# Graph layers with 36 buffers for fetched rows and gathered tiles in fewer batches

## The chip, the cores and the metric

One core of one Trainium2 chip runs the whole kernel. The metric is the time of one execution on the device in microseconds, median of three runs: 1799.24 (1791.07 to 1801.76).

## The reference

The graph has 3125 nodes with 256 features and 50,000 edges, sorted by destination. With `norm[e] = dis[src] * dis[dst]` (from the degrees), three layers follow:

```python
def tagconv(x, src, dst, norm, W, b):
    out = x @ W[0]
    h = x
    for k in range(1, 4):
        h = segment_sum(norm[:, None] * h[src], dst, N)
        out = out + h @ W[k]
    return out + b
h = relu(tagconv(x, ..., W1, b1)); h = relu(tagconv(h, ..., W2, b2))
return layernorm(x + tagconv(h, ..., W3, b3))
```

## The kernel before, in words

**The form of the work.** The adjacency commutes with the weights, so a layer is evaluated as a nested sum: V3 = g W3, then three hops, V(k) = g W(k) + A V(k+1) for k = 2, 1, 0. Each value is held as a pair of float16 halves, high and low, so a row of V has 512 columns. There are 25 tiles of 128 nodes (the last has 53 rows). A hop is called (L, k), with layer L = 0, 1, 2; k = 3 is the first projection of a layer. The nine hops follow one another, since each needs all of the V before it.

**Dense and gathered tiles.** In a hop, 19 tiles (`DENSE`, indices 0 to 18) are dense: four projection matmuls (L1266, L1268) and then 25 matmuls of the adjacency in fp8 against V in SBUF (L1405, and L1410 for the last block). Tile 24, which has few rows, is dense too, with its own operand AT (L1383 to L1387), except in the three hops of `LONG`, (0,2), (0,0) and (1,0), where it is gathered. Tiles 19 to 23 are always gathered. Their edges are taken in steps: five steps a tile (`GV`), four windows of 128 edges a step, each window serving 32 destination rows. A window needs 128 rows of V: an indirect DMA on GpSimd's queue (L942) fetches them from the copy of V in HBM (`vh`) into a slot of the buffer GB. TensorE multiplies them by a one-hot selection SG (L1319; L1316 for tile 24), four matmuls of 32 columns side by side, one for each window. The fifth step of a tile needs only two fetches, since two windows share one, so a tile is 18 fetches; tile 24 is 9. A hop has 90 fetches, a long one 99.

**The order.** `schedule()` writes out one list for all engines. In it the gathered steps stand in batches behind dense tiles: the tables `FIRST` (hop (0,2)), `LONGER` (the other long hops), `LAST` (hop (2,0)) and `STEPS` (the rest) say behind which dense index how many steps of `sequence` are done. In hop (0,2) the order of steps is tiles 19, 20, 24, 21 to 23; in the other long hops tile 24 comes first. Behind each dense tile of a hop with k = 0 the list also has the transposition ("T") and the first projection ("P", L+1, 3) of tiles that are finished, for the next layer.

**Fetches.** GpSimd's loop issues the fetches in the order of the steps. It starts a hop once the 25 tiles of V of the hop before are stored by SyncE (`keep`, L700; semaphores `s_vd`). `ring()` deals out the slots of GB in turn; a fetch waits until the step that used its slot before is done on TensorE. There are 24 slots, of which 16 are in use in hop (0,2), as the other 8 hold comparison patterns until then. On TensorE each gather matmul waits for the semaphore of its slot.

**PSUM.** Bank 7 takes each gathered tile (its projection, then its steps). Dense tiles rotate over banks 0, 1, 2, 5, 6 (in (0,2) over 0, 1, 2). Before a bank is used again `emptied()` waits for VectorE. In layer 0 the projection of a tile ("S", `started`, L1285, L1291) is done inside the dense tile before, and ScalarE scales it in place (L977); `gather` waits for that. In layers 1 and 2 `gather` projects a tile itself, at its first step.

**Behind a tile** ScalarE scales the low half (L1120), VectorE adds (L1789), ScalarE writes the high half of V (L1090) and VectorE the low half (L1761), and VectorE takes maxima for a later check of ranges (L1632). In the last hop (2,0) VectorE forms the output (L1837, L1839; L1831, L1833 for the last tile) and the layer normalisation, with a chain of small operations from L1843 to L1859 and two steps on ScalarE (L1135, L1031). The 23rd and 24th tile in the order share one such chain (`members`). ScalarE takes up the next tile after it has scaled the output of the one before.

## Time and profile before

| | us |
|---|---|
| median of three runs | 1799.24 |
| lowest, highest | 1791.07, 1801.76 |
| span of the profiled execution | 1250.4 |
| TensorE busy | 1224.4 (98%) |
| GpSimd busy | 850.6 (68%) |
| VectorE busy | 629.7 (50%) |
| ScalarE busy | 397.2 (32%) |
| granted TensorE clock, mean | 0.993 |

The profile page gives one execution from its first to its last instruction, the span. The time of a run is longer than that; the page does not give the whole time of the execution that it profiles, so its span stands beside the median of the runs, 548.8 us above it. Engines are named PE (TensorE, with PEld for its weight loads), DVE (VectorE), ACT (ScalarE), POOL (GpSimd) and SP (SyncE). L1319 is line 1319 of the kernel before. Times in rows are microseconds from the span's start, unless a column says ns.

### The profile page before, as it was taken

What the parts mean: (1) busy time and instruction counts of PE and PEld (TensorE: products, weight loads), DVE (VectorE), ACT (ScalarE), POOL (GpSimd) and SP (SyncE); (2) the same over time, 40 slices, a digit from 0 to 9 for tenths busy, and PEclk for the clock granted to TensorE, in tenths of its full rate; (3) what the DMA queues carried; (4) which work ended last, traced back from release to release, by engine and by line L of the source; (5) the groups of instructions that cost most, each with busy time, mean ns of one, the idle gap of its engine ahead of it and who ended that gap; (6) DMA issues with size and microseconds to landing.
All of it is one profiled execution on the core that took longest, in us unless ns stands there. A gap on an engine that the chain in (4) does not pass through costs nothing.

```text
span 1250.4 us, 19518 instructions
## 1 busy us (share of the span) xinstructions
PE 1224.4 (98%) x7413; PEld 610.2 (49%) x7413; DVE 629.7 (50%) x1552; ACT 397.2 (32%) x916; POOL 850.6 (68%) x937
## 2 busy tenths in 40 slices
PE   5999999999999999999999999999999999999997
PEld 4655554444444444444444454444444544454444
DVE  7876664444455555433443345555433433345655
ACT  6676774422233331111221122222111111112222
POOL 8677775777477755776577657773777477747773
PEclk8999999999999999999999999999999999999999
DMA  5343443544255553444354435553444344435553
GB/s 182 111 124 107 115 124 101 156 135 135 79 142 157 146 126 104 131 130 125 108 156 132 122 97 150 149 149 94 131 130 128 102 129 130 131 92 151 153 162 93
DMA packets 110070, 160.05 MB, mean 128 GB/s; under 512 B 43719, under 2 KB 82225, under 8 KB 109970
## 3 DMA queue, kind: packets, MB, share of 16 engines
q0 software_dynamic: 40480, 110.54, 31.6%
q1 hardware_dynamic: 69416, 48.13, 12.8%
q8 instruction: 61, 1.00, 0.3%
q14 instruction: 39, 0.32, 0.1%
q10 hardware_dynamic: 74, 0.05, 0.0%
HBM read 120.51 MB, written 32.10 MB: 122 GB/s over the span
## 4 chain that ended last, share of the span: by engine, by line
PE 88%; POOL 5%; DVE 3%; issue 2%; ACT 1%; DMA 1%; POOLq 0%; DVEq 0%; ACTq 0%
PE pb L1405 65%; PE pb L1266 6%; POOL GB L942 4%; PE pb L1319 4%; PE pb L1268 3%; PE pb L1285 3%; PE pb L1161 2%; PE pb L1410 1%; PE pb L1291 1%; PE pb L1383 1%; PE pb L1194 0%; DVE V L1744 0%; POOL gT L825 0%; DMA GB<-vh,KS 0%; DVE gT L1503 0%
## 5 line engine op out<-in xcount | busy, mean ns | idle before, releaser
L942 POOL DMA_INDIRECT GB<-vh,KS x837 | 807.9, 965 | 371.2 <-issue 246.2
L1405 PE MATMUL pb<-V,A 128*128 128x512 f16 x4104 | 944.8, 379 | 0.0
L1405 PEld LDWEIGHTS pb<-V,A 128*128 128x128 fp8e4 x4104 | 395.3, 98 | 429.5 <-issue 5.2
L1789 DVE SCALAR_TENSOR_TENSOR pb<-pb,cst,t 128x256 f32<-128x256 f32 (+1 forms) x200 | 97.7, 488 | 357.8 <-ACT t L1120 357.8
L1120 ACT ACTIVATE t<-pb,cst 128x256 f32<-128x256 f32 (+1 forms) x224 | 105.2, 469 | 441.8 <-PE pb L1410 398.0
L1266 PE MATMUL pb<-Whl,gT 128*128 128x512 f16 x384 | 134.2, 380 | 1.2 <-DVE gT L1730 1.2
L1761 DVE SCALAR_TENSOR_TENSOR V<-V,pb 128x256 f16<-128x256 f16 (+1 forms) x200 | 83.8, 421 | 82.1 <-ACT V L1090 81.5
L1090 ACT ACTIVATE V<-pb 128x256 f16<-128x256 f32 (+1 forms) x200 | 75.9, 383 | 127.3 <-DVE pb L1789 127.2
L1268 PE MATMUL pb<-Whl,gT 128*128 128x256 f16 x384 | 104.7, 273 | 0.0
L1632 DVE TENSOR_REDUCE stat<-V 128x1 f32<-128x256 f16 x225 | 91.3, 412 | 0.2
L1780 DVE TENSOR_REDUCE ast<-A 128x1 f32<-128x610 uint8 x100 | 77.8, 778 | 0.0
L1010 ACT ACTIVATE A<-pb 128x500 fp8e4<-128x500 f32 x122 | 71.1, 585 | 18.2 <-PE pb L1161 17.4
L1794 DVE SCALAR_TENSOR_TENSOR w<-bb,cst,t 128x256 f32<-128x256 f32 (+1 forms) x50 | 24.2, 485 | 80.4 <-ACT t L1120 80.4
L1266 PEld LDWEIGHTS pb<-Whl,gT 128*128 128x128 f16 x384 | 37.5, 98 | 55.0 <-issue 10.3
L1319 PE MATMUL pb<-GB,SG 128*32 128x512 f16 x900 | 58.8, 381 | 0.3 <-DMA GB<-vh,KS 0.3
L977 ACT ACTIVATE pb<-pb,cst 128x512 f32<-128x512 f32 (+1 forms) x75 | 48.5, 650 | 28.3 <-PE pb L1291 28.1
L1161 PE MATMUL pb<-GB,Whl 128*128 128x125 f16 x499 | 50.8, 225 | 2.1 <-DVE GB L1613 1.8
L1161 PEld LDWEIGHTS pb<-GB,Whl 128*128 128x128 f16 x499 | 38.6, 100 | 29.1 <-issue 5.0
L1410 PE MATMUL pb<-V,A 128*128 128x256 f16 x171 | 46.6, 273 | 0.0
L1611 DVE TENSOR_TENSOR Whl<-Whl,GB 128x1024 f16<-128x1024 f16 x63 | 43.4, 688 | 4.4 <-PE pb L1161 3.8
L1285 PE MATMUL pb<-Whl,gT 128*128 128x512 f16 (+1 forms) x150 | 44.5, 379 | 0.3 <-ACT AT L1010 0.3
L1120 ACT ACTIVATE t<-pb 128x256 f32<-128x256 f32 (+1 forms) x50 | 19.1, 382 | 80.3 <-PE pb L1410 73.5
(227 smaller groups left out, 687.8 us busy)
## 6 DMA issues: line engine op xcount, KB each, us to landing
vh<-V SPq DMA_DIRECT2D x216, 128.0 KB
GB<-vh,KS POOLq DMA_INDIRECT x837, 2.8
xr<-in_x SPq DMA_DIRECT2D x24, 128.0 KB, 3.0
out<-g SPq DMA_DIRECT2D x24, 128.0 KB, 1.9
xr<-in_W SPq DMA_DIRECT2D x22, 128.0 KB, 2.4
V<-in_xt SPq DMA_DIRECT2D x5, 512.0 KB, 6.1
gT<-w SPq DMA_TRANSPOSE x46
V<-in_xt SPq DMA_DIRECT2D x1, 640.0 KB, 3.8
```

The costliest lines, as they stand in the source:

```text
L942: pool.indirect_dma_start(GB[:, slot, :], None, vh[vbuf[(L, k + 1)]][:, :], bass.IndirectOffsetOnAxis(ap=KS[:, p:p + 1], axis=0))\
L1120: act.activation(t1[0:r, e % RB, :], lo, ACT.Copy, scale=sc).then_inc(S["s_a1"], 1)
L1161: mm = pe.matmul(BB[gi % 2][:, k * KEYS:(k + 1) * KEYS], OB[:, b % NO, vis % BV // VL, :, vis % VL], OK[:, b % NO, vis % BV // VL, :, vis ...
L1266: pe.matmul(acc[:, :], gT[:, t, c, 0, :], Whl[:, L % 2, c, k, :], start=(c == 0), stop=False, skip_group_check=True)
L1268: mm = pe.matmul(acc[:, F:512], gT[:, t, c, 1, :], Whl[:, L % 2, c, k, 0:F], start=False, stop=(k == 3 and c == 1), skip_group_check=True)
L1285: pe.matmul(high, gT[:, t, c, 0, 0:r], Whl[:, 0, c, k, low], start=(c == 0), stop=False, skip_group_check=True)
L1319: mm = pe.matmul(acc[GH * j:GH * j + GH, :], SG[:, p, :], GB[:, slot, :], start=False, stop=last_step(st), skip_group_check=True)
L1405: mm = pe.matmul(acc[:, :], A8[:, a, t * P:(t + 1) * P], src[:, a, :], start=False, stop=(n == NT - 1), skip_group_check=True)
L1632: dve.tensor_reduce(stat[:, col:col + 1], ap, axis, ALU.max, apply_absolute_value=True).then_inc(S["s_st"], 1)
L1761: dve.scalar_tensor_tensor(lo, vb[0:r, t, 0:F], -SC, hi, ALU.mult, ALU.add).then_inc(S["s_v"], 1)
L1780: dve.tensor_reduce(ast[:, nam:nam + 1], A8[:, a_, NC // 4 * i_:NC // 4 * (i_ + 1)].bitcast(U8), AX.X, ALU.max).then_inc(S["s_st"], 1)
L1789: dve.scalar_tensor_tensor(hi, hi, cst[0:r, 1, t:t + 1], lt, ALU.mult, ALU.add).then_inc(S["s_d1"], 1)
```

## The change

GB gets 36 slots in place of 24, 28 of them in use in hop (0,2) and the 8 lent ones from hop (0,1) on. The room comes from the space for descriptors of dynamic DMAs, which is set to 4096 bytes a partition. The semaphores of six earlier loads serve a second time for slots 30 to 35. The four tables are written anew: hop (0,2) has 6 batches in place of 11, hops (0,0) and (1,0) 4 in place of 6, the other six hops 3 in place of 5. A batch can now hold the steps of two or three tiles; `openers()` lists the tiles that open in a batch, and `gather` projects (or, in layer 0, waits for) all of them at the batch's first step. Gathered tiles alternate between banks 6 and 7 (7 alone in hop (0,2)), and dense tiles rotate over 0, 1, 2, 5. At most two first projections of the next layer stand behind a dense tile; more are left for the next one.

```diff
@@ -45,10 +45,11 @@
 LONG = ((0, 2), (0, 0), (1, 0))
 WG = WIN // GRAN
 FULL = (GV - 1) * WG
-NSLOT, NFIRST = 24, 16
+NSLOT, NFIRST, NLENT = 36, 16, 8
+SCRATCH = 4096
 SGW = 18
-FIRST = {3: 2, 5: 5, 6: 7, 8: 10, 9: 15, 11: 17, 12: 20, 14: 22, 15: 25, 16: 27, 18: 30}
-STEPS = {4: 5, 8: 10, 11: 15, 15: 20, 19: 25}
+FIRST = {4: 5, 7: 10, 8: 15, 11: 20, 14: 25, 18: 30}
+STEPS = {7: 8, 12: 15, 19: 25}
 JZ = 1536
 HP = 125
 HN = N // HP
@@ -65,8 +66,8 @@
 SPREAD = 17
 RULED = 24
 OUTSIDE = 4096.0
-LONGER = {2: 5, 5: 10, 8: 15, 12: 20, 15: 25, 18: 30}
-LAST = {4: 5, 8: 10, 11: 15, 15: 20, 18: 25}
+LONGER = {5: 10, 10: 18, 15: 25, 18: 30}
+LAST = {7: 8, 12: 15, 18: 25}
 LAG = 3
 LATER = (0, 2, 5, 9, 10, 15)
 AHEAD = 9
@@ -138,9 +139,9 @@
                     out += [("S", 0, k, tile_of(st)) for st in sequence(L, k)[at:steps.get(i, at)] if st % GV == 0]
                 out.append(("P", L, k, t))
                 if k == 0 and L < 2:
-                    out += [("P", L + 1, 3, c) for c in fresh]
-                    fresh = done[turned:]
-                    out += [("T", L + 1, c) for c in fresh]
+                    out += [("P", L + 1, 3, c) for c in fresh[:2]]
+                    fresh = fresh[2:] + done[turned:]
+                    out += [("T", L + 1, c) for c in done[turned:]]
                     turned = len(done)
                 done.append(t)
                 for s in sequence(L, k)[at:steps.get(i, at)]:
@@ -203,17 +204,30 @@
 
 def ring(sched):
 
-    slots, use, before = list(range(NFIRST)), {}, {}
+    slots, use, before = [*range(NFIRST), *range(NFIRST + NLENT, NSLOT)], {}, {}
     out = {}
     for L, k, s in (it[1:] for it in sched if it[0] == "G"):
-        if (L, k) == (0, 1) and len(slots) == NFIRST:
-            slots = list(range(NFIRST, NSLOT)) + slots
+        if (L, k) == (0, 1) and len(slots) < NSLOT:
+            slots = list(range(NFIRST, NFIRST + NLENT)) + slots
         for d, _ in fetches(s):
             b = slots.pop(0)
             slots.append(b)
             use[b] = use.get(b, 0) + 1
             out[fetched(L, k) + d] = (b, use[b], before.get(b))
             before[b] = (L, k, s)
+    return out
+
+
+def openers(sched):
+
+    out, run = {}, None
+    for it in sched:
+        if it[0] == "G":
+            run = run or it[1:]
+            if it[3] % GV == 0:
+                out.setdefault(run, []).append(tile_of(it[3]))
+        elif not (it[0] == "P" and it[2] < 3 and it[3] not in dense(*it[1:3])):
+            run = None
     return out
 
 
@@ -576,7 +590,7 @@
         xT = v1.bitcast(F32)
         W3 = g[:, 0:2, :]
         w1 = Whl[:, 1, :, :, :].rearrange("p c k n -> p (c k n)")
-        g2 = GB[:, NFIRST:NSLOT, :].rearrange("p a b -> p (a b)")
+        g2 = GB[:, NFIRST:NFIRST + NLENT, :].rearrange("p a b -> p (a b)")
         OB = w1[:, 0:NO * P * BV].rearrange("p (r u j v) -> p r u j v", r=NO, u=BV // VL, v=VL)
         iotaB = w1[:, 3072:3072 + P * VL].rearrange("p (j v) -> p j v", v=VL)
         KKb = w1[:, 3328:3328 + QK * P]
@@ -611,10 +625,12 @@
             few = (L, k) == (0, 2) or (L, k) == (0, 3) and not 10 <= t < 17
             if (L, k) == (0, 3) and t < len(PAIRED):
                 b = PAIRED[t]
-            elif (L, k, t) == (0, 2, 0) or k < 3 and t not in dense(L, k):
+            elif k < 3 and t not in dense(L, k):
+                b = 6 if (L, k) != (0, 2) and t < NT - 1 and (t - TD) % 2 == 0 else 7
+            elif (L, k, t) == (0, 2, 0):
                 b = 7
             else:
-                b = next(i for i in free if not few or i < 5)
+                b = next(i for i in free if (not few or i < 5) and (i < 6 or (L, k) == (0, 3)))
                 free.remove(b)
                 free.append(b)
             bank_of[e] = b
@@ -649,9 +665,10 @@
         s_x = [sem(f"s_x{i}") for i in range(len(XC) - 1)]
         s_ol = [sem(f"s_ol{i}") for i in range(RB)]
         s_msg = [sem(f"s_msg{i}") for i in range(9 * NQ)]
-        s_gl = [sem(f"s_gl{i}") for i in range(QW + 1)]
+        s_landed = [sem(f"s_landed{i}") for i in range(QW + 1)]
+        s_gl = s_landed
         s_vd = [sem(f"s_vd{i}") for i in range(2)]
-        s_gb = [sem(f"s_gb{i}") for i in range(NSLOT)]
+        s_gb = [sem(f"s_gb{i}") for i in range(NSLOT - len(s_landed))] + s_landed
         split = [w[:, i, :].bitcast(F16).rearrange("p (c h m) -> p c h m", c=2, h=2) for i in range(2)]
 
         def landings(L, t):
@@ -1292,24 +1309,31 @@
                                    skip_group_check=True)
                 mm.then_inc(S["s_pj"], 1)
 
+            OPENED = openers(SCHED)
+
+            def opened(L, k, t):
+
+                e = pe_no[(L, k, t)]
+                if L == 0:
+                    pe.wait_ge(S["s_pm"], s_no[(L, k, t)] + 1)
+                    return
+                emptied(p_of[user[e]])
+                if t == NT - 1:
+                    tail(L, k, PB[e])
+                else:
+                    project(L, k, t, PB[e])
+
             def gather(L, k, st):
 
                 t = tile_of(st)
-                e = pe_no[(L, k, t)]
-                acc = bank[7]
-                if st % GV == 0 and L == 0:
-                    pe.wait_ge(S["s_pm"], s_no[(L, k, t)] + 1)
-                elif st % GV == 0:
-                    emptied(p_of[user[e]])
-                    if t == NT - 1:
-                        tail(L, k, acc)
-                    else:
-                        project(L, k, t, acc)
+                acc = PB[pe_no[(L, k, t)]]
+                for other in OPENED.get((L, k, st), ()):
+                    opened(L, k, other)
                 for j, (d, p) in enumerate(multiplied(st)):
                     if (L, k) == (0, 2):
                         pe.wait_ge(S["s_s5"], 3 + p // SGW)
                     slot, use, _ = RING[fetched(L, k) + d]
-                    pe.wait_ge(s_gb[slot], 16 * use)
+                    pe.wait_ge(s_gb[slot], 16 * (use + (slot >= NSLOT - len(s_landed))))
                     if t == NT - 1:
                         for m in range(2):
                             at = HALF * m + GH * j
@@ -1867,7 +1891,7 @@
     from concourse import mybir as _mybir
     from concourse.bass_utils import run_bass_kernel_spmd as _run
 
-    nc = _bacc.Bacc("TRN2", target_bir_lowering=False, num_devices=1)
+    nc = _bacc.Bacc("TRN2", target_bir_lowering=False, num_devices=1, dynamic_dma_scratch_size=SCRATCH)
     src = _np.asarray(inputs["src"])
     dst = _np.asarray(inputs["dst"])
     pad = _np.full(WIN, -1, _np.int32)
```

## Rows read from the trace of the kernel before

**Rows 1.** Part 1 of the page: busy us (share of the span) and instructions.

```profile
PE 1224.4 (98%) x7413; PEld 610.2 (49%) x7413; DVE 629.7 (50%) x1552; ACT 397.2 (32%) x916; POOL 850.6 (68%) x937
```

**Rows 2.** Stretches: length, then busy us of PE, PEld, DVE, ACT, POOL; clock, DMA.

```profile
60.00:1238.00 1178.00, 1176.12 (x6982) 575.26 (x6981) 574.69 (x1406) 352.61 (x805) 806.89 (x836) 1.00 0.45 128
1238.00:1250.40 12.40, 4.95 (x79) 3.60 (x77) 6.86 (x24) 3.01 (x7) 0.00 (x0) 0.80 0.10 31
```

**Rows 3.** Waits of TensorE for fetched rows: us in total, times, longest us.

```profile
PEld pb L1319 <- DMA GB<-vh,KS: 1.8, 4, 0.8
...
PE pb L1319 <- DMA GB<-vh,KS: 0.3, 1, 0.3
```

**Rows 4.** The fetch line: ns min/median/max of an issue, and us to landing.

```profile
L942 POOL DMA_INDIRECT GB<-vh,KS x837: 940/946/3077, 58.8 to 1233.1; - x168
...
DMA to landing us min/median/max: 2.6/2.8/4.6
```

**Rows 5.** Timeline of PE around a batch in hop (1,2): start us, us, line.

```profile
573.27 0.27 PE L1268 MATMUL pb<-Whl,gT 128*128 128x256 f16 x1
573.47 1.26 PE L1319 MATMUL pb<-GB,SG 128*32 128x512 f16 x20
574.66 0.39 PE L1266 MATMUL pb<-Whl,gT 128*128 128x512 f16 x1
```

**Rows 6.** Timeline of PE: L1405 of two dense tiles in succession.

```profile
575.33 5.34 PE L1405 MATMUL pb<-V,A 128*128 128x512 f16 x24
...
581.26 5.34 PE L1405 MATMUL pb<-V,A 128*128 128x512 f16 x24
```

**Rows 7.** Timeline of PE in (0,2): end of dense tile 8; tile 24's gather.

```profile
119.91 0.27 PE L1410 MATMUL pb<-V,A 128*128 128x256 f16 x1
...
129.23 0.73 PE L1316 MATMUL pb<-GB,SG 128*32 128x256 f16 x20
```

**Rows 8.** Timeline of POOL in hop (0,2): fetches 25, 36 and 45.

```profile
96.34 0.95 POOL L942 DMA_INDIRECT GB<-vh,KS  x1 [3.25 <-PE pb L1319]
...
111.51 0.95 POOL L942 DMA_INDIRECT GB<-vh,KS  x1 [0.30 <-issue]
...
124.30 0.97 POOL L942 DMA_INDIRECT GB<-vh,KS  x1 [0.30 <-issue]
```

**Rows 9.** Timeline of PE: last batch of (0,1), and index 5's of (0,0).

```profile
328.24 1.26 PE L1319 MATMUL pb<-GB,SG 128*32 128x512 f16 x20
...
370.51 1.26 PE L1319 MATMUL pb<-GB,SG 128*32 128x512 f16 x20
```

**Rows 10.** Costliest groups, VectorE's maxima: busy us, mean ns, idle us before.

```profile
L1632 DVE TENSOR_REDUCE stat<-V 128x1 f32<-128x256 f16 x225 | 91.3, 412 | 0.2
```

**Rows 11.** Timeline: first fetches of (0,0) and (1,2), last of (1,2), last batch.

```profile
334.88 0.94 POOL L942 DMA_INDIRECT GB<-vh,KS  x1 [14.98 <-DMA vh<-V]
...
478.23 0.94 POOL L942 DMA_INDIRECT GB<-vh,KS  x1 [18.28 <-DMA vh<-V]
...
589.47 0.95 POOL L942 DMA_INDIRECT GB<-vh,KS  x1 [0.30 <-issue]
...
596.52 1.26 PE L1319 MATMUL pb<-GB,SG 128*32 128x512 f16 x20
```

**Rows 12.** Timelines of DVE and PE at the end, in order of time.

```profile
1225.53 0.16 DVE L1859 SCALAR_TENSOR_TENSOR lnb<-lnb 128x1 f32<-128x1 f32 x1
...
1226.79 0.48 DVE L1837 SCALAR_TENSOR_TENSOR g<-pb,cst,t 128x256 f32<-128x256 f32 x1 [0.73 <-ACT t L1120]
...
1229.65 0.16 DVE L1859 SCALAR_TENSOR_TENSOR lnb<-lnb 128x1 f32<-128x1 f32 x1
...
1237.65 0.27 PE L1410 MATMUL pb<-V,A 128*128 128x256 f16 x1
...
1238.55 0.49 DVE L1837 SCALAR_TENSOR_TENSOR g<-pb,cst,t 128x256 f32<-128x256 f32 x1 [2.58 <-ACT t L1120]
...
1243.75 0.49 DVE L1831 SCALAR_TENSOR_TENSOR t<-pb,cst,w 64x256 f32<-64x256 f32 x1
```


## The prediction

> **What bounds the kernel now.** I read the busy time of each engine first: TensorE is busy for 98% of the span, GpSimd for 68% [rows 1]. An average can hide a stage with another limit, so the second view cuts the span into start, middle and end: between 60 and 1238 us TensorE is busy for 1176.1 of 1178 us, at full clock, and at the end it stops at about 1243 while VectorE works on [rows 2]. The reader is to see that no wait in the middle is worth more than 1.9 us together: time there can be gained only by giving TensorE less to do. The third view is the waits: TensorE has waited for fetched rows for 0.3 us, and its weight loads for 1.8 us, in five places [rows 3]. The fourth is the fetch line on GpSimd: 837 fetches of 0.946 us, one every 1.25 us with the issue gap, each landing 2.8 us (at most 4.6) after its issue [rows 4]. So a hop of 90 fetches takes GpSimd 112 us out of the hop's 126 (19 tiles by 5.94, five gathered ones by 1.94 with projection and change of form, some 3 for tile 24), and it can start only when the hop before is stored. GpSimd is off the path, but by little, and that is where the change can lose what it gains.
>
> The page gives the span of the profiled execution, 1250.4 us, and not its whole time. The median of the three runs is 548.8 us longer. I carry that part unchanged: my sum is a difference of spans, laid on the median of 1799.2.
>
> **Fewer batches.** Before, the gathered steps stand in 53 batches: 11 in hop (0,2), 6 each in (0,0) and (1,0), 5 in each of the other six. After there are 32: 6, 4, 4 and 18. No matmul is added or removed. What goes is the change of TensorE between its 128-column and 32-column forms. In hop (1,2) a batch of 20 gather matmuls starts 0.20 us after a matmul whose own pace is 0.107, and the next projection starts 1.19 us later, while five rounds of four parallel matmuls at 0.213 are 1.07 [rows 5]. So one batch costs 0.10 + 0.12 = 0.22 us beside its work, and 21 batches fewer give **-4.6 us**, all of it on the path, since TensorE is never idle there. [...] The bounds of this term are near: 0.20 to 0.25.
>
> **Waits for rows that go.** In the hops with five batches the first one came after 5 dense tiles and needed 18 fetches; now it comes after 8 and needs 30. A dense tile is 5.94 us [rows 6], so the engine comes 17.8 us later and the fetches 15 us later: 2.8 us of slack more, and likewise for the old third batch. I take **-1.0 us** for this, between the 0.3 and 2.1 of [rows 3]. Later on the slack stays: 54 fetches are now wanted after 13 tiles and not after 12.
>
> **The ring of buffers.** With 36 slots fetch n waits for the use of fetch n-36. In a hop with batches of 30, 24 and 36 fetches the 37th is issued about 5 + 45 = 50 us into the hop, and the first batch runs from 48.8 us on (8 tiles and two projections). The waits are met, or nearly; the last batch needs 36 rows, exactly the ring. I cost this at nothing. Its cover is GpSimd's lead: if it goes, each us of delay comes out in the last batch of the hop.
>
> **Hop (0,2).** Here the lead is short. Tile 24's steps move from dense index 9 to index 8, and they need fetch 45. Before, TensorE did them at 129.2 us and ended index 8 at 120.0 [rows 7]. Now it ends index 8 at about 120.4 (three more gathered steps before it, one batch fewer). Fetch 45 was issued at 124.30, in a stream that had lost 3.25 us to a wait for a slot [rows 8]. With 28 slots in place of 16 that wait goes, so it is issued at 121.05 and lands at 123.9, wanted at 121.0: a stall of 2.8 us, and 0.3 more at index 11, where fetch 63 is wanted. I take **+3.1 us**. Bounds: 0.5 (GpSimd's slower rows, of which this hop has most, fall elsewhere: the issue takes 0.940 at best and 3.077 at worst [rows 4]) to 5 (a landing of 4.6).
>
> **Hops (0,0) and (1,0).** The first batch, at index 5, is now the double one: tiles 24 and 19 on 27 fetches. Hop (0,0) starts at 329.4, where the gather that began at 328.24 ends, and its index-5 batch began at 370.51 [rows 9]. One batch (0.73), one projection of the next layer (0.65) and a 0.1 fall out before it, so it begins at 369.0 and wants its last row at 370.4. GpSimd started at 334.88 [rows 11]. It will start 0.9 us later: three tiles now end almost together before the hop (24, 22, 23) and VectorE needs about 2.6 us for each, six operations of 0.41 to 0.49 like those of [rows 10]. Fetch 27 then lands at 335.8 + 32.8 + 2.8 = 371.4: a stall of 1.0, and 0.2 at index 10. In (1,0) fewer of those operations stand before the start, GpSimd begins about 1 us nearer to it, and I find no stall. **+1.2 us**, bounds 0 and 5 (both hops, landings of 4.6 at each of two batches).
>
> Hop (1,2) has the longest wait for the stores of V, 18.3 us before its first fetch [rows 11]. The 30 fetches of its first batch are issued by 514.5 and landed by 517.3. The hop began near 471.5 (its last gather ends at 597.7, 126 later), so the batch comes at 519: safe by 2 us.
>
> **Two banks, one bank fewer for dense tiles.** Dense tiles rotate through four banks, not five. A bank is drained some 3 us after its tile and asked for again after four tiles, 24 us: nothing. Three ACT scalings instead of two behind tile 24 in layer 0 could hold TensorE 0.2 us once: nothing. At most two projections of the next layer now stand between dense tiles, so they spread and do not grow.
>
> **The end.** VectorE is the path from 1238 on. Tile 18 ends on TensorE at 1237.92; VectorE takes it up at 1238.55 and, tile 23 between, tile 24 at 1243.75 [rows 12]. The pair that shares one normalisation chain is the 23rd and 24th in order: before tiles 18 and 23, after it 22 and 23. Tile 18 then has a chain of its own. Such a lone tile holds up the next one for 4.1 us: 3.02 from 1226.79 to the end of 1229.65's row, and 1.10 from a chain's last row (ends 1225.69) through ScalarE's two steps to the next start at 1226.79 [rows 12]. So after tile 18's end the last tile is taken up at 0.63 + 4.12 + 5.20 = 9.9 us in place of 5.8 (5.20 is the pair, 1238.55 to 1243.75): 4.1 later. Against this, tile 18 itself ends 1.7 us earlier, as tile 22's projection (0.65, 574.66 to 575.33 in [rows 5, 6]) and gather (1.07) move behind it. **+2.4 us**; bounds 0 and 4.
>
> **Sum:** -4.6 - 1.0 + 3.1 + 1.2 + 2.4 = +1.1 us, so 1800.3. [...]
>
> **Rivals.**
> (a) *The whole gain arrives.* No new stall, and the end is hidden: 1799.2 - 5.6 = 1793.6. For it: TensorE is nearly never idle, and my stalls come from margins of 1 us. Against: fetch 45 would have to land 2.8 us sooner, and the end is a plain chain of rows.
> (b) *The fetches fall behind more.* Landings near 4.6 at every double batch and later hop starts carried on: some 1.8 us at each of 5 tight batches beyond my sum, so 1800.3 + 9 = 1809. For it: stores of V move in the same stretches. Against: the median landing is 2.8.
> [...]
> (d) *The change does not do what it says in time*: the 548.8 us outside the span move with the different layout, to either side. Nothing in the profile speaks for it; at 2%, 1763 or 1835.
>
> **How the numbers follow.** My forecast 0.55, (a) 0.24, (b) 0.11, (c) 0.06, (d) 0.04. Adding the bounds gives -6.2 to +9.1, or 1793 to 1808. The three runs lie 8 below and 3 above their median, and a new median can do so too; with (a) and (b) the range is 1788 to 1812. (c) and (d) are left out. One per cent, 18 us, is about what a measurement of this kernel tells from no change. No case but (d) gives faster by 1%: 0.03 with an allowance; (c), half of (d) and the tail of (b) give slower 0.08; within 0.89.
>
> **What would show it.** Right: batches of about 1.7, 1.5 and 2.3 us in the ordinary hops and TensorE's L1319 rows in 32 places; a wait of TensorE for fetched rows near 121 us; the last tile's L1831 about 10 us after tile 18's last matmul, not 6. [...] A median beyond 1812 or under 1788 would break the sum.

## The result, and the profile after

The changed kernel takes 2049.09 us (median of 6 runs, 2044.95 to 2059.12) against 1794.99 us for the kernel before beside it (1791.07 to 1801.76): ratio 1.141, interval 1.1375 to 1.1438. It is 14% slower, where 1800.3 in 1788 to 1812 was forecast.

The profiled execution of it took 2044.95 us for a span of 2043.2. So 1.75 us lie outside the span, and the picture is another than that of [rows 1]: the page's busy row, the granted clock in 40 slices, the engines' share of the chain that ended last, the three groups that matter, and the longest waits of GpSimd (us in total, times, longest).

```profile
PE 1403.7 (69%) x7413; PEld 633.1 (31%) x7413; DVE 628.6 (31%) x1552; ACT 398.6 (20%) x916; POOL 842.9 (41%) x937
...
PEclk8787896887877797877797777869678967896788
...
PE 58%; issue 21%; another core or an unknown queue 13%; DVE 4%; ACT 3%; POOL 1%; DMA 0%; ACTq 0%; POOLq 0%; DVEq 0%
...
L1429 PE MATMUL pb<-V,A 128*128 128x512 f16 x4104 | 1093.2, 408 | 402.1 <-issue 302.9
L959 POOL DMA_INDIRECT GB<-vh,KS x837 | 799.8, 956 | 1142.4 <-PE pb L1343 548.3
L1429 PEld LDWEIGHTS pb<-V,A 128*128 128x128 fp8e4 x4104 | 410.5, 102 | 965.9 <-issue 503.1
```

```profile
POOL GB L959 <- PE pb L1343: 548.3, 20, 42.7
PEld pb L1429 <- issue: 503.1, 535, 3.4
...
POOL GB L959 <- DMA vh<-V: 300.4, 9, 44.8
```

TensorE is busy for 69%, not 98%, and the idle time before the dense matmuls (L1405 before, L1429 now) is put down to "issue": the engine waited for nothing that the profile shows. GpSimd's fetches are as cheap as in [rows 4] (0.956 us); it waits for TensorE's gather (L1343), 20 times.

The timeline shows what happens. TensorE in hop (1,2): start us, us, line, and idle time before.

```profile
906.51 0.27 PE L1285 MATMUL pb<-Whl,gT 128*128 128x256 f16 x1
906.72 1.69 PE L1343 MATMUL pb<-GB,SG 128*32 128x512 f16 x28
908.34 0.39 PE L1283 MATMUL pb<-Whl,gT 128*128 128x512 f16 x1
...
914.94 5.34 PE L1429 MATMUL pb<-V,A 128*128 128x512 f16 x24
...
920.88 0.38 PE L1429 MATMUL pb<-V,A 128*128 128x512 f16 x1
923.35 0.38 PE L1429 MATMUL pb<-V,A 128*128 128x512 f16 x1 [2.09 <-issue]
924.78 0.58 PE L1429 MATMUL pb<-V,A 128*128 128x512 f16 x1 [1.05 <-issue]
...
937.42 0.59 PE L1429 MATMUL pb<-V,A 128*128 128x512 f16 x1 [2.23 <-issue]
938.82 0.58 PE L1429 MATMUL pb<-V,A 128*128 128x512 f16 x1 [0.82 <-issue]
940.22 5.29 PE L1429 MATMUL pb<-V,A 128*128 128x512 f16 x13 [0.81 <-issue]
```

GpSimd at the same time: the first and the last of 24 fetches that it issues 1.25 us apart.

```profile
907.64 0.95 POOL L959 DMA_INDIRECT GB<-vh,KS  x1 [20.97 <-PE pb L1343]
...
936.46 0.94 POOL L959 DMA_INDIRECT GB<-vh,KS  x1 [0.30 <-issue]
```

And the two stretches of that run, cut where TensorE changes pace (length, busy us of PE, PEld, DVE, ACT, POOL; clock, DMA share, GB/s):

```profile
907.64:921.26 13.62, 13.62 (x79) 6.21 (x71) 5.34 (x12) 1.92 (x5) 10.44 (x11) 1.00 0.42 125
921.26:940.20 18.94, 5.64 (x10) 1.14 (x11) 1.71 (x4) 0.38 (x1) 12.32 (x13) 0.57 0.36 104
```

For 13.6 us from the first fetch TensorE runs at full pace. Then its matmuls start 1.4 to 2.8 us apart, in steps of 0.70 us; with the weight load between, that is at best an instruction in 0.70 us. It stays so until the last fetch has landed (936.46 issued, full pace from 940.22), and in 18.9 us it does ten matmuls. The granted clock is 0.57 in that stretch and 0.50 from 924 to 938 us, where TensorE is busy for 4.7 of 14 us. I call it a *slow stretch*, and fetches issued without a pause a *run*. The trace after has 33 runs, of 36, 30 and 24 fetches in an ordinary hop, and nearly every one has its slow stretch.

### The profile page after: what moved, and what is told of

The parts are those of the page before. It is cut to its first block, busy times and chain, and to the rows that moved or that the text cites. A ratio compares the mean times of both kernels' runs of the same rounds, so it can differ in the third digit from the quotient of the medians.

```text
span 2043.2 us, 19514 instructions
## 1 busy us (share of the span) xinstructions
PE 1403.7 (69%) x7413; PEld 633.1 (31%) x7413; DVE 628.6 (31%) x1552; ACT 398.6 (20%) x916; POOL 842.9 (41%) x937
## 3 DMA queue, kind: packets, MB, share of 16 engines
q0 software_dynamic: 40480, 110.54, 19.0%
## 4 chain that ended last, share of the span: by engine, by line
PE 58%; issue 21%; another core or an unknown queue 13%; DVE 4%; ACT 3%; POOL 1%; DMA 0%; ACTq 0%; POOLq 0%; DVEq 0%
PE pb L1429 44%; PE pb L1283 4%; PE pb L1285 2%; PE pb L1343 2%; PE pb L1302 1%; PE pb L1178 1%; PE pb L1434 1%; PE pb L1308 1%; PE pb L1407 1%; ACT t L1137 1%; ACT A L1027 1%; DVE pb L1813 1%; DVE stat L1656 0%; ACT V L1107 0%
## 5 line engine op out<-in xcount | busy, mean ns | idle before, releaser
L1429 PE MATMUL pb<-V,A 128*128 128x512 f16 x4104 | 1093.2, 408 | 402.1 <-issue 302.9
L959 POOL DMA_INDIRECT GB<-vh,KS x837 | 799.8, 956 | 1142.4 <-PE pb L1343 548.3
L1429 PEld LDWEIGHTS pb<-V,A 128*128 128x128 fp8e4 x4104 | 410.5, 102 | 965.9 <-issue 503.1
L1283 PE MATMUL pb<-Whl,gT 128*128 128x512 f16 x384 | 141.0, 396 | 42.1 <-issue 36.8
L1285 PE MATMUL pb<-Whl,gT 128*128 128x256 f16 x384 | 108.4, 282 | 35.8 <-issue 35.5
L1302 PE MATMUL pb<-Whl,gT 128*128 128x512 f16 (+1 forms) x150 | 48.6, 408 | 55.3 <-DVE V L1785 34.9
L1343 PE MATMUL pb<-GB,SG 128*32 128x512 f16 x900 | 54.3, 380 | 0.0
```

What stands on the lines that cost most here:

```text
L959: pool.indirect_dma_start(GB[:, slot, :], None, vh[vbuf[(L, k + 1)]][:, :], bass.IndirectOffsetOnAxis(ap=KS[:, p:p + 1], axis=0))\
L1283: pe.matmul(acc[:, :], gT[:, t, c, 0, :], Whl[:, L % 2, c, k, :], start=(c == 0), stop=False, skip_group_check=True)
L1285: mm = pe.matmul(acc[:, F:512], gT[:, t, c, 1, :], Whl[:, L % 2, c, k, 0:F], start=False, stop=(k == 3 and c == 1), skip_group_check=True)
L1343: mm = pe.matmul(acc[GH * j:GH * j + GH, :], SG[:, p, :], GB[:, slot, :], start=False, stop=last_step(st), skip_group_check=True)
L1429: mm = pe.matmul(acc[:, :], A8[:, a, t * P:(t + 1) * P], src[:, a, :], start=False, stop=(n == NT - 1), skip_group_check=True)
```

## The experiments

Theory A: a run of GpSimd's fetches leaves TensorE about 14 us at full pace and slows it from there until the run has landed. The execution profiled of the kernel before had no slow stretch although its fetches ran for 112 us without a pause; its ordinary executions would have them, and the 548.8 us are inside their span.

**The kernel before, once more.**

> The kernel before, unchanged, for a profile of an ordinary execution: the profiled one had a span of 1250.4 us, the timed ones took 1795. Theory A (crawl): once GpSimd has issued fetches without a pause for some 14 us, TensorE gets its instructions only every 0.7 us until the last of them has landed; the lost time goes by the length and number of these runs of fetches. It then expects a span near 1793, a mean clock near 0.85, about 46 stretches of slow TensorE in 46 runs of fetches, each beginning 13 to 15 us after a run begins, and each run ending in a wait of GpSimd for a slot. Theory B (descriptor space): the kernel before has no such stretches; a span near 1250 beside a run time of 1795 would then mean that 545 us lie outside the span.

1797.05 us, span 1795.3. Its busy row and clock; then one run of 18 fetches from 896.23, cut as above.

```profile
PE 1404.6 (78%) x7413; PEld 637.4 (36%) x7413; DVE 629.6 (35%) x1552; ACT 398.3 (22%) x916; POOL 845.6 (47%) x937
...
PEclk8998998888797898889888988889887988897879
```

```profile
896.23:910.90 14.67, 14.53 (x79) 6.55 (x71) 6.51 (x14) 3.95 (x11) 11.32 (x12) 1.00 0.51 147
910.90:921.00 10.10, 3.93 (x10) 0.73 (x9) 0.00 (x0) 0.00 (x0) 5.95 (x7) 0.74 0.34 100
```

The same picture. The ordinary execution of before has 54 runs (24, 18, 18, 18, 12 in a hop; 46 in all were expected). The trace that the prediction read was not one of them.

**The descriptor space alone**, in the kernel before:

```diff
+nc = _bacc.Bacc("TRN2", ..., dynamic_dma_scratch_size=4096)
```

> The kernel before with the descriptor space of dynamic DMAs set to 4096 bytes, and nothing else: 24 buffers, old batches. Theory A: no change, 1795 within 1%. Theory B: the smaller space is what costs, so about 2049, and at least a third of the 254 us.

1789.83 us, ratio 0.9965 (0.9946 to 0.9983). The smaller space costs nothing, and GpSimd's 784 gaps before a fetch that the profile puts down to "issue" are 0.3 us at most: rival (c), by which the smaller space holds GpSimd up, falls.

**The buffers without the tables**: the changed kernel with `FIRST`, `STEPS`, `LONGER` and `LAST` of before.

> The changed kernel with the four tables of batches of the kernel before: 36 buffers, 4 KB, two banks, 53 batches. Theory A: with 36 buffers the first run of a hop grows from 24 to 36 fetches and the number of runs in a hop falls from 5 to 4, in nine hops; each pause saved costs about 12 us (254 us for 21 batches), so about 1900. Theory T (the tables alone, with the long batches and their double projections): 1795. Theory B: 2049.

1883.12 us, ratio 1.0485 (1.045 to 1.052). With 36 slots the first run of a hop is 36 long and swallows the second: 36, 18, 18, 18, some 44 runs. So about a third of the loss comes with the buffers (this kernel also keeps the change of banks and the limit of two first projections behind a dense tile, which no run takes alone), two thirds with the tables, which make it 33 runs.

**Runs cut to 9**, in the kernel before:

```diff
                             .then_inc(s_gb[slot], 16)
+                        run += 1
+                        if run % DRAIN == 0:
+                            pool.wait_ge(s_gb[slot], 16 * use)
```

> The kernel before, and GpSimd waits after every ninth fetch of a hop until that fetch has landed, before it issues the next. Theory A: runs of 9 fetches last 11 us and end before the slow stretch would begin; a pause of 3 us may be long enough to renew the start. Then a hop is bound by GpSimd, 10 times (11.3 + 2.8) = 141 us and its start, nine hops about 1330 and 65 before them: about 1400. If a pause of 3 us is too short: 1795 or somewhat more. Theory B and any theory in which fetches are only late: GpSimd loses 25 us in each hop, so slower than 1795, near 1850.

1489.35 us, ratio 0.8296 (0.8273 to 0.8319), with one added wait on GpSimd, though not the 1400 us that were reckoned: from one hop to the next it takes 144 to 184 us. Its busy row; GpSimd around a pause; the run of nine between two pauses:

```profile
PE 1315.2 (89%) x7413; PEld 620.4 (42%) x7413; DVE 630.9 (43%) x1552; ACT 396.8 (27%) x916; POOL 850.6 (58%) x937
```

```profile
738.20 0.95 POOL L943 DMA_INDIRECT GB<-vh,KS  x1 [0.30 <-issue]
741.23 0.95 POOL L943 DMA_INDIRECT GB<-vh,KS  x1 [2.09 <-issue]
```

```profile
728.20:741.20 13.00, 12.98 (x76) 6.06 (x78) 4.73 (x10) 2.72 (x8) 8.51 (x9) 1.00 0.47 132
```

A pause of 3.0 us from issue to issue, and TensorE keeps its pace. Same matmuls, same fetches: what cost the time was the unbroken run.

**The changed kernel with the same wait.**

> The changed kernel whole (36 buffers, 4 KB, longer batches, two banks), and in it GpSimd waits for the landing of every 9th fetch of a hop before it issues the next, as in the kernel before with that wait, which took 1489.35 us. Theory A (what the change costs is only that GpSimd's unbroken runs of fetches get longer, and TensorE issues an instruction in some 0.7 us from about 14 us into a run until it has landed): with all runs cut to 9 fetches the two kernels come out nearly alike, 1465 to 1515 us, the difference being the small terms of my sum (+1.1 us, between -7 and +10). Rival R (the longer batches themselves hold TensorE up, since buffers come free later and its first matmul waits longer): the changed kernel stays over 5% behind, 1570 us or more.

1486.69 us, ratio 0.8245 (0.8206 to 0.8284): level with the kernel before under the same wait, whose interval it overlaps. Rival R falls here: with runs of the same length the 14% are gone.

**Every 6th and every 3rd**, in the kernel before (`DRAIN = 6`, `DRAIN = 3`).

> The kernel before, with GpSimd waiting for the landing of every 6th fetch in place of every 9th (1489.35 us). Theory A: the short slow stretches that were left with 9 (some 110 us of idle TensorE in them) mostly go, since a run of 6 lasts about 6.3 us and is landed at 9; each pause costs GpSimd some 1.8 us, 15 of them in a hop in place of 10, 9 us a hop on an engine that has slack in most hops. 1400 to 1480 us. Rival Q (it is not how long a run lasts, the waits helped only because they moved the fetches to another place against the batches): no clear gain on 9, 1480 to 1560 us.

1459.35 us, ratio 0.8122 (0.8091 to 0.8152), in the range. Before the dense matmuls no idle time is put down to "issue" any more (208.0 us in the ordinary execution of before, 48.6 with every 9th). What TensorE waits for now is rows: 88.1 us in 94 waits.

> The kernel before, with GpSimd waiting for the landing of every 3rd fetch. Theory A: no slow stretch is left (a run of 3 is landed 5 us after its first issue), but GpSimd now needs 3.8 us x 30 = 114 us and 30 pauses of 1.8 us = 54 us in a long hop, 168 us against the 147 us that a hop takes with every 9th, so GpSimd is the bound: 1500 to 1620 us with the mean granted clock of TensorE no lower than with 9 (0.95). Rival Q: slow stretches go on, the clock stays below 0.95.

1710.52 us, ratio 0.9513 (0.948 to 0.9546): above the range, and the clock was 0.881, not 0.95. Now TensorE waits for rows far more than the 2.1 us of [rows 3]. The gather matmuls, and GpSimd's fetches:

```profile
L943 POOL DMA_INDIRECT GB<-vh,KS x837 | 805.7, 963 | 835.0 <-DMA GB<-vh,KS 577.4
...
L1323 PE MATMUL pb<-GB,SG 128*32 128x512 f16 x900 | 167.0, 438 | 265.6 <-DMA GB<-vh,KS 264.5
```

GpSimd is the bound: from the first to the last fetch of an ordinary hop it takes 162 to 167 us, as reckoned (168). What I left out are the 8 us until the next hop can start (16 behind (0,0) and (1,0)) and the 20 to 30 more that hops (0,2), (0,0) and (1,0) take. The clock fell where TensorE waits for rows: 0.74 from 720 to 740 us, with 8.7 us of such waits, and 1.00 from 740 to 760, where it is always busy. Before TensorE's dense matmuls the profile has no idle time from "issue", so there are no slow stretches.

**A wait two behind**: after each issue GpSimd waits for the landing of the fetch two before it.

```diff
+                        sent.append((slot, use))
+                        if len(sent) > 2:
+                            pool.wait_ge(s_gb[sent[-3][0]], 16 * sent[-3][1])
```

> The kernel before, and from the third fetch of a hop on GpSimd waits, after each issue, for the landing of the fetch issued two before it. At most three are ever under way, but the queue never runs empty as long as a run lasts (a landing comes about 2.8 us after its issue, and issues are 1.25 us apart). Theory A1 (what counts is that the queue runs empty now and then): slow stretches as before, 1750 to 1850 us. Theory A2 (what counts is a backlog of fetches that builds up in a run until it holds up TensorE's instructions): no backlog can build up, the slow stretches go, and the time comes to 1400 to 1520 us.

1749.52 us, ratio 0.9728 (0.9696 to 0.9759). The added wait hardly ever holds GpSimd up (the profile puts 8.4 us in 11 waits down to landings): in a run it goes on issuing 1.25 us apart, so each fetch has landed by the time that it is asked for. The slow stretches stay, and no backlog of fetches is behind them (A2 falls). Why this kernel is 2.7% faster is not shown.

**What starts a slow stretch.** Two kernels leave work out, a third issues the dense columns in twice as many instructions:

```diff
 # every second gather matmul left out, the last step excepted
+                    if j % 2 == 0 and not last_step(st):
+                        continue
 # 64 rows a fetch from a slot's second use on
+                        rows = P if use == 1 else P // 2
+ pool.indirect_dma_start(GB[0:rows, slot, :], ..., ap=KS[0:rows, p:p + 1])
 # each dense matmul as two of 256 columns
+                            for m in range(2):
+                                mm = pe.matmul(acc[:, F * m:F * (m + 1)], ..., src[:, a, F * m:F * (m + 1)], ...)
```

> The kernel before, and in a gathered tile's steps but the last TensorE leaves out every second matmul (12 of 20 in a tile are left, so its output is not the reference's). Fetches, waits and batches are as before. Asked is what starts a slow stretch. Theory T (the time or the number of fetches since a run of GpSimd began): slow stretches start 13 to 15 us and some 11 fetches into a run, as before, though fewer of TensorE's instructions lie between. Theory I (the number of TensorE's instructions since then, 120 to 150 in the runs before, as if a store of fetched instructions were used up that isn't filled again while fetches go on): they start later by about the share left out, at 18 us or more, and the short runs of 12 and 18 show none.

1742.28 us (one run; before beside it 1757.44). It could not tell: so few of the instructions of a run are gather matmuls that the slow stretch came after as many as before, at 16.4 us. That short runs would show none was a miss.

> The kernel before, and a fetch into a buffer that has been used before brings 64 rows in place of 128 (rows 64 to 127 of the buffer keep what they held, so the output is not the reference's). Half the descriptors and half the bytes a fetch; GpSimd's time for one should fall from 0.95 us. Theory D (the descriptors or bytes queued are what starts and feeds a slow stretch): a slow stretch starts only after some 22 fetches of a run, so that runs of 12 and 18 show none, and within one TensorE's instructions come faster than one in 0.7 us; total well below 1700 us. Theory T (time since the run began): starts at 13 to 15 us whatever the fetch brings. Theory N (the number of instructions on GpSimd's queue): starts after 11 fetches, earlier in time.

1821.1 us (one run; before beside it 1757.44). Half the rows and half the bytes a fetch (57.26 MB on the fetches' queue in place of 110.54) gain nothing, and the slow stretch starts as early as before: D falls.

> The kernel before, with each dense 128x512 matmul (4104) issued as two of 256 columns, each with its weight load: the same columns multiplied in twice as many of TensorE's instructions, GpSimd's fetches as before. Theory T (the time since a run of GpSimd's fetches began, 13 to 15 us): slow stretches start where they did, 13 to 15 us in. In them an instruction still takes some 0.7 us, so the stretches, whose end GpSimd sets, get half as many columns done. Total 1800 to 1950 us. Theory I (the number of TensorE's instructions since the run began: it was 110 to 177 in every slow stretch of the runs so far, at 0.1 us each mostly, and where TensorE waited between, 25 or 30 us passed before it was reached): slow stretches start when some 140 of the doubled instructions are through, 7 to 9 us and 6 to 8 fetches into a run, the runs of 12 are slow too, and each of some 50 runs costs 6 us more on top: 2050 to 2400 us.

2044.77 us (one run; before beside it 1761.44), 5 us under the range of theory I. One run of each, up to the slow stretch and into it, in this order:

```profile
914.50:930.90 16.40, 16.16 (x81) 7.31 (x77) 5.23 (x11) 1.90 (x5) 12.45 (x14) 1.00 0.42 120
930.90:939.50 8.60, 2.67 (x7) 0.81 (x8) 0.00 (x0) 0.00 (x0) 4.52 (x5) 0.69 0.32 91
```

```profile
949.67:963.50 13.83, 13.83 (x77) 6.37 (x69) 5.23 (x11) 1.90 (x5) 10.47 (x12) 1.00 0.29 81
963.50:975.00 11.50, 3.72 (x8) 0.80 (x8) 0.00 (x0) 0.00 (x0) 5.71 (x7) 0.70 0.15 41
```

```profile
1494.34:1502.20 7.86, 7.86 (x74) 6.06 (x66) 3.29 (x7) 1.05 (x3) 6.03 (x7) 1.00 0.42 119
1502.20:1519.00 16.80, 6.26 (x24) 2.09 (x23) 0.49 (x1) 0.74 (x2) 11.02 (x12) 0.59 0.36 101
```

The last pair decides. With twice as many instructions the stretch starts at 7.9 us and 7 fetches, not at 14.7 and 12, but after about as many of TensorE's instructions: 74 + 66 = 140 against 79 + 71 = 150. Theory I holds, T falls, and so does N, a count of fetches. The median over the runs from hop (1,2) on, instructions counted by their starts, says much the same (where exactly a slow stretch starts can be read within 1 us): 14.6 us and 140 instructions before, 13.6 and 143 after, 16.2 and 153 with gather matmuls left out, 13.9 and 134 with half rows, 7.9 and 128 split. The small differences fit a store that in a run goes down by one for each instruction and is made up by one in 0.70 us, the pace of the slow stretch. From the rows: 150 - 14.67/0.70 = 129 for the kernel before, 140 - 7.86/0.70 = 129 for the split one, 131 for the changed kernel, 126 for half rows, 135 for the kernel with matmuls left out. That is a model that fits five kernels, not a thing seen.

**A shorter pause**: the wait after every 9th fetch is for the 8th.

> The kernel before, and after every 9th fetch of a hop GpSimd waits for the landing of the 8th, not of the 9th: a pause of some 1.9 us from issue to issue in place of 3, and the 9th fetch is still under way when the wait ends, so the queue is hardly ever empty. If only an empty queue lets TensorE's instructions be fetched again (A1): as without a wait, 1730 to 1820 us. If a pause of GpSimd itself is enough (A3): as with the full wait or better, 1440 to 1520 us.

1637.46 us, ratio 0.931 (0.9238 to 0.9381; before beside it 1761.44), between both theories. The pause is 1.70 us from issue to issue (731.82 to 733.52). It is neither that only an empty queue helps nor that any pause will do; in the model, a shorter pause makes up part of the store.

**The changed kernel with every 6th.**

> The changed kernel, with GpSimd waiting for the landing of every 6th fetch. With every 9th the changed kernel (1486.69 us) and the one before (1489.35 us) came out alike; with every 6th the one before took 1459.35 us. Theory A, by which the change costs nothing but longer runs: alike again, 1445 to 1475 us. If 36 buffers let GpSimd get ahead where it is what is waited for (it is 34% of the chain of waits there): 1435 to 1455 us. Rival R (the longer batches cost by themselves where GpSimd is close to being the bound): over 1475 us.

1492.16 us, ratio 0.8465 (0.8406 to 0.8525; before beside it 1761.44). The kernel before had 1459.35 with this wait, ratio 0.8122, with 1798.26 beside it. So by times the changed kernel is 2% slower and by ratios 4%, and the time lies in rival R's range. TensorE waits 113.2 us for rows, 25 more than the kernel before with this wait, and in hop (0,0) another 10.3 us, in five waits, for VectorE to empty a bank. The starts of the hops (first fetch, us from one hop to the next) show where:

```
                       (0,2) (0,1) (0,0) (1,2) (1,1) (1,0) (2,2) (2,1)
before, every 9th      184.2 155.7 172.2 143.8 145.7 171.1 144.7 147.3
changed, every 9th     196.1 147.2 194.7 141.6 143.4 180.9 140.4 143.1
before, every 6th      169.2 148.6 171.2 145.1 147.3 170.1 145.7 145.5
changed, every 6th     175.8 149.5 174.9 150.6 153.9 174.8 149.1 148.5
```

By these rows long hops seem to like the old tables and short runs, ordinary hops the new tables and runs of 9. The next kernel puts that to the test.

**Each hop its better form**: the changed kernel with the old `FIRST` and `LONGER`, and waits by hop.

```diff
+DRAIN = {(0, 2): 6, (0, 0): 6, (1, 0): 6}
+                        if run % DRAIN.get((L, k), 9) == 0:
```

> The changed kernel with a wait for every 9th fetch in the six ordinary hops and for every 6th in (0,2), (0,0) and (1,0), and with the batch tables FIRST and LONGER of before for these three. From the hops' starts in the traces: with the changed tables and every 9th the ordinary hops take 140.4 to 143.4 us (143.8 to 147.3 with the tables of before, 148.5 to 153.9 with every 6th), while the three long ones are shortest with the old tables and every 6th (169.2, 171.2, 170.1 against 196.1, 194.7, 180.9). Added up, 58 + 169 + 147 + 171 + 142 + 143 + 170 + 140 + 143 + about 150 for the last hop and the end = 1433. If the parts add (theory A: a hop's time is that of its own runs and batches): 1415 to 1450 us. If hops are not independent (how many of TensorE's instructions are left over from the hop before decides): 1460 us or more.

1447.15 us, ratio 0.8064 (0.8036 to 0.8092), in the range, but the parts did not add as I had it. From one hop's first fetch to the next the ordinary hops take 139.3 to 145.7 us, as reckoned. The long ones take 176.0, 176.0 and 175.7, not 169, 171 and 170, and the changed kernel with the new tables and every 6th had 175.8, 174.9 and 174.8. So the tables are not what makes the long hops longer. What is left is the rest of the change, the slots, the banks and the limit on first projections, and no run separates these. One place shows in the trace, again in hop (0,0), where L1306 is the projection that the kernel before has in L1285 (us in total, times, longest):

```profile
PE pb L1306 <- DVE V L1789: 10.2, 5, 2.7
```

The kernel beats the one before by 19%. It had the lowest time, but its interval touches that of the kernel before with every 6th (0.8091 to 0.8152), which needs only the added wait. Its busy row:

```profile
PE 1297.4 (90%) x7413; PEld 624.3 (43%) x7413; DVE 632.6 (44%) x1552; ACT 397.3 (27%) x916; POOL 849.7 (59%) x937
```

## Why the prediction was wrong

**The step that failed** is the one ahead of the sum: "I carry that part unchanged". It took the 548.8 us between span and median for something outside the work, and the profiled execution for a picture of the rest. The runs show that an ordinary execution of before spans 1795.3 us, 1.75 below its own time, 545 us more than the trace that I read: TensorE is idle for 365 us more of them and busy for 180 more, at a lower clock, with slow stretches in most of its runs. Rival (d) named the gap and gave it 0.04, because nothing in the profile spoke for a move. But a span 30% short of the runs was itself the sign: the trace could not show where a third of the time went, and a range of 1788 to 1812 had no ground.

**"I cost this at nothing. Its cover is GpSimd's lead"** The ring is where the loss enters. Fetching goes on for 837 x 1.25 = 1046 us however it is cut, and each run gives TensorE only its first 14 us. Longer batches and 36 slots give fewer, longer runs: 54, 44, 33. One hop, (1,1), before and after, has the same busy time of TensorE in 25 us more:

```profile
852.20:1032.00 179.80, 145.72 (x728) 62.13 (x726) 51.47 (x108) 27.11 (x66) 85.35 (x90) 0.87 0.31 90
```

```profile
975.70:1180.70 205.00, 145.81 (x728) 61.88 (x727) 51.50 (x108) 26.85 (x66) 85.30 (x90) 0.80 0.27 79
```

The changed hop has three runs, each with a fresh start, and the one before has five. The other hops lose 20 to 42 us each (first fetch to first fetch), 248 us in all between these two executions, where the medians are 254 apart.

**The batches' change of form, -4.6 us**: right in size. In the changed kernel the 28 gather matmuls start at 906.72, 0.10 after the pace of the row before, and the next projection 1.62 us later, for seven rounds of 0.213 = 1.49: 0.10 + 0.13 = 0.23 a batch, where 0.22 was used. It is 1.8% of what the change cost.

**The waits for rows, -1.0, +3.1 and +1.2 us**: not there. The changed kernel's gather matmuls have no idle time for rows at all; TensorE is so late that every fetch has long landed. Only where runs are short are there such waits, 25 us more with every 6th in the changed kernel than in the one before. The 3.7 to 6.6 us that its long hops take more there do not come from the batches, as the last kernel shows.

**One bank fewer for dense tiles, "nothing"**: under the slow stretches it can't be seen. Where they are gone, TensorE waits for VectorE to empty a bank for 10 us in hop (0,0), so this term was not nothing.

**The end, +2.4 us**: one of its two parts can be checked. Tile 18's last dense matmul and the first VectorE row of the last tile, in the changed kernel:

```profile
2026.97 0.27 PE L1434 MATMUL pb<-V,A 128*128 128x256 f16 x1
```

```profile
2037.20 0.49 DVE L1855 SCALAR_TENSOR_TENSOR t<-pb,cst,w 64x256 f32<-64x256 f32 x1
```

9.96 us between them, where 9.9 was forecast and [rows 12] had 5.8, as has the ordinary execution of before. The lone chain of tile 18 costs its 4.1 us.

**The descriptor space, rival (c), 0.06**: that 4096 bytes would hold GpSimd up was my estimate, from no row. No run shows it: with that space alone the kernel before takes 0.9965 of its time.

**The bounds.** The sum of the bounds leaves out those of the batches; with 21 times 0.20 and 0.25 it runs from -6.9 to +9.5, which helps nothing here.

**What is held up.** A count of instructions fits two things: TensorE's supply of instructions, or the way out of what each finished one leaves. The traces speak for the second. In the ordinary execution of before, the last matmul of a tile and the start of ScalarE's work on that tile:

```profile
908.51 0.27 PE L1410 MATMUL pb<-V,A 128*128 128x256 f16 x1
...
921.94 0.47 ACT L1120 ACTIVATE t<-pb,cst 128x256 f32<-128x256 f32 x1 [14.91 <-remote]
```

The same tile in the execution of [rows 1]:

```profile
641.14 0.27 PE L1410 MATMUL pb<-V,A 128*128 128x256 f16 x1
...
641.45 0.47 ACT L1120 ACTIVATE t<-pb,cst 128x256 f32<-128x256 f32 x1 [3.77 <-PE pb L1410]
```

ScalarE follows after 0.31 us there, and after 13.4 us here, some 4 us behind the last fetch of the run (917.7), though it is idle all the while. By its record the matmul is over at 908.8, but its signal comes late; "remote" says that the profile finds no instruction that had just ended. It is so throughout. The execution of [rows 1] has no such wait of L1120, and the ordinary one has this (us in total, times, longest):

```profile
ACT t L1120 <- remote: 665.0, 76, 24.9
```

From the start of a tile's last matmul to ScalarE's start, where ScalarE was idle, it is never over 0.43 us in the execution of [rows 1]. In the ordinary one it is over 1 us for 71 tiles, and up to 21.2; with every 9th fetch waited for the longest is 12.1 us, with every 6th 6.4 and with every 3rd 2.6. The model of a store says nothing of these signals. The tile before, whose last matmul starts 6.4 us into the run, is taken up 2.3 us later; if each instruction since the run's start had to go out ahead of it at one in 0.70 us, it would take far longer.

As to TensorE's supply, the profile has a DMA queue that it names `instruction`: 61 packets of 16 KB, one for some 250 of TensorE's instructions, and 93 in the split kernel, 32 more for its 8208 further instructions. They take a median of 0.97 us in the execution of [rows 1] and of 1.00 us in the ordinary one. In the split kernel seven of them fall into slow stretches from hop (1,2) on, and they take 0.88 to 1.47 us. The slow stretches of the ordinary execution start anywhere from about 4 to 236 instructions behind the last such packet. So no packet of that queue is seen to come late.

**Left open.** Why the signals come late, and whether that and the slow pace are one thing. Nor is it known why the one execution shown of before was free of both. One difference is in the traces themselves. That of [rows 1] holds 22,654 records of semaphore updates, 19,136 of them of DMAs; that of the ordinary execution, of the same program, holds 8930 and 5976. So the second lacks more than half of them. Each execution whose span is known here was recorded by the profiler. That the recording takes part in the slow stretches is a rival that no run tests, and what the kernels take without it is not shown.

## What to carry to other kernels

Set the span of the profile beside its own time, and both beside the median of the runs, before reading any share; if they don't meet, the trace is of something else, and the first step is to get another. A long unbroken run of indirect DMAs from GpSimd can slow TensorE by a factor of seven per instruction (0.70 us where it is some 0.10 at full pace) with no wait to be seen: look for signals that come late and count TensorE's instructions from the start of a run; here it helped to let GpSimd stop for 3 us every 6 to 9 fetches (0.8122 and 0.8296 of the time). Before a kernel is built around that, its time should be taken once without the profiler. More buffers for fetches are no gain by themselves, since they let a run grow (36 slots with the old tables: 1.0485).

## What the runs showed of the hardware

- In the ordinary executions, not in that of [rows 1]: while GpSimd issues indirect DMAs of 128 rows of 1 KB every 1.25 us, TensorE keeps its pace for some 130 to 150 instructions (14 us; 7.9 us with matmuls of 256 columns), then issues at best one in 0.70 us until 3 to 4 us after the last issue.
- Its signals come late in such a run: 2.3 and 13.4 us from a tile's last matmul to ScalarE's start, where 0.31 us is usual. The 16 KB packets of the queue `instruction` do not take long: 0.88 to 1.47 us in slow stretches of the split kernel, with a median of 1.00 us over the whole ordinary execution of before.
- Half the rows and bytes a fetch did not help: with 64 rows a fetch (0.91 us in place of 0.96 on GpSimd) it starts as early (13.8 us), and the one run takes 1821 us.
- Three fetches under way at most are enough to keep it going (1749.52 us); after a pause of 3.0 us from issue to issue, with all landed, TensorE has its full pace again (busy for 12.98 of 13.00 us); one of 1.7 us, which leaves a fetch under way, does so in part (1637.46 us, where 1489.35 is the time with the full pause).
- The granted clock goes down to 0.50 of full speed within a slow stretch (924 to 938 us; a mean of 0.57 and 0.59 in two of the windows above), and TensorE's same work makes it busy for 1404 us against 1224 of [rows 1], 15% more.
- 4 KB for descriptors of dynamic DMAs did not slow 837 fetches of 128 rows (0.9965).
